# Normalisation, cosines and sines, and the first query weights ahead of an attention: a preparation stage rewritten

## The chip, the cores and the metric

The kernel runs on one core of one Trainium2 chip. The metric is the device time of one execution in microseconds, from the first to the last of its work on that core. TensorE multiplies, VectorE (DVE in the rows), ScalarE (ACT) and GpSimd (POOL) do element-wise work, and SyncE (SP) issues the transfers.

## What is computed

Four layers of a gated text model: for each, `x = x + tanh(g) * attention(layernorm(x))` and then `x = x + tanh(g) * ffn(layernorm(x))`. x has 32 x 64 tokens of 512 numbers (f32), which the kernel holds as 16 tiles of 128 tokens. The change lies at the entry of the fourth attention, which has 32 query heads and 8 key heads of size 128 and rotates queries and keys by their positions:

```python
cos_t, sin_t = _rope_tables(MAX_POS, D, ROPE_THETA)     # 512 positions x 128
cos = cos_t[position_ids][:, None]
sin = sin_t[position_ids][:, None]
q = q * cos + _rotate_half(q) * sin
k = k * cos + _rotate_half(k) * sin
...
scores = jnp.where(mask == 0, jnp.float32(-1000000000.0), scores)
```

In each table the second 64 columns repeat the first 64 (`concatenate([freqs, freqs])`).

## The kernel before

The program has four stages, one behind the other, each a block over all engines that ends in a barrier: `prepare_weights`, `early_layers` (three layers and their ffns, and the fourth attention's keys and values), `prepare_last` (L1489) and `last_attention` (L1641). `early_layers` leaves x in DRAM (`x_mid`), k and v too. Behind each stage GpSimd clears the stage's semaphores one by one (`stage`), and a barrier follows; at the start of the next, GpSimd raises the semaphores of the PSUM banks (`banks.open`, L277 and L278), two for each bank.

`prepare_last` fills what the last attention reads: `X` (x itself, 16 tiles), `xTh` and `xTl` (the normalised x, transposed and split into two bf16 halves), `cos` and `sin` (128 x 2048 f32, head dimension on the partitions), `mask`, and the first `raw_q` and `raw_o` (weights of the first four query heads). SyncE issues seven transfers in this order: the positions, copied to all 128 partitions; the table of cosines (512 x 128) and that of sines; all of x; the mask; raw_q; raw_o. VectorE turns positions to f32 and clamps them in four passes over 128 x 2048 (L1585 to L1591), and then makes four turns, each over four tiles (512 tokens). In a turn VectorE takes the statistics of four tiles (`bn_stats` L1604, `bn_aggr` L1607), GpSimd makes 1/sqrt(var + eps) for each tile in two operations (L1544, L1547), VectorE normalises (L1610, `xn`), TensorE transposes (L1565), ScalarE rounds to bf16 (L1577, `xTh`), and VectorE takes the rest (L1616, `xTl`). A position is looked up by a product: VectorE compares the positions with the row numbers (`hot`, L1599, four operations for a turn, into one buffer `one_hot`), and TensorE multiplies the table with that (L1558), in f32, cosines and then sines, each four products of 128x128 by 128x512; ScalarE copies the two results out (L1574). VectorE's order in a turn is statistics, normalise, `hot` of the next turn, `xTl`; TensorE's is cosines, sines, transposes. The mask comes last (L1626).

`last_attention` runs eight turns, one for each key head. Before its loop ScalarE rounds raw_q to `wqh` and GpSimd takes the rest, `wql`, in four pieces q0 to q3 (L1934, L2040). TensorE waits for q0's `wql` and projects queries (`project_q` by `three`, L349 to L351, twelve bf16 matmuls); VectorE multiplies by cos and sin (`rotate`, L2093 to L2095), and GpSimd adds the two parts (L2035). The list `FIRST` holds the projections and rotations that go ahead of the loop. From the second key head on, wqh and wql are made inside the loop, and this stays as it is.

## Time and profile before

| | us |
|---|---|
| median of 3 runs (2362.61 to 2378.12) | 2366.32 |
| the profiled execution, device time | 2366.56 |
| its span, first to last instruction | 2364.5 |
| TensorE busy | 1939.2 (82%) |
| VectorE busy | 1702.7 (72%) |
| ScalarE busy | 559.1 (24%) |
| GpSimd busy | 609.7 (26%) |
| granted TensorE clock, mean | 0.894 of full |

A row of the trace has a start and a duration in us from the span's start, the engine, the line of the kernel, the operation and, for a wait, how long the engine had been idle and what released it. `prepare_last` covers about 1244 to 1308 us of the span; TensorE's first matmul of the last attention stands at 1311.20 us.

### The profile page before, as it was taken

Reading aid. Unit: us, or ns where it says so; the run is one execution under the profiler, and the core shown is the slowest. Engines: PE = TensorE matmul, PEld = TensorE weight load, DVE = VectorE, ACT = ScalarE, POOL = GpSimd, SP = SyncE. Lnnn points to the kernel's source line nnn. Section 1 sums busy time; section 2 is a strip of 40 time slices with the busy share of each in tenths; the row PEclk is TensorE's granted clock in tenths of the full one; section 3 lists DMA queues with packets and bytes.
Section 4 is the critical chain, followed back from the end, with each engine's and each line's share of the span. In section 5 each row is a group of like instructions: output and inputs, shape, how many; then the busy total and the mean of one; then the engine's idle time right before and its main releaser. Section 6 shows DMA issues by size and latency. Waiting matters only on the chain. (4 is left out here: it accounts for less than half of the span.)

```text
span 2364.5 us, 40599 instructions
## 1 busy us (share of the span) xinstructions
PE 1939.2 (82%) x14722; PEld 1103.0 (47%) x14872; DVE 1702.7 (72%) x3005; ACT 559.1 (24%) x1326; POOL 609.7 (26%) x728
## 2 busy tenths in 40 slices
PE   4587879877898788887766798989899989898876
PEld 2343556435653455544543354545454545454432
DVE  4489655895459954698536788878788878887875
ACT  2221223222332223222221222222222222222221
POOL 0310213002230103201012434333334343434220
PEclk7699778997699986999857999999999999999987
DMA  7357202461043700453004212021212021200100
GB/s 228 134 139 202 63 2 82 125 188 54 1 127 111 204 8 1 131 158 106 1 18 142 72 28 62 28 61 27 63 28 62 27 62 27 62 27 27 31 24 36
DMA packets 134552, 176.08 MB, mean 74 GB/s; under 512 B 46304, under 2 KB 73568, under 8 KB 134288
## 3 DMA queue, kind: packets, MB, share of 16 engines
q1 hardware_dynamic: 134416, 174.20, 24.9%
q8 instruction: 94, 1.54, 0.3%
q14 instruction: 42, 0.34, 0.0%
HBM read 132.09 MB, written 42.07 MB: 74 GB/s over the span
## 5 line engine op out<-in xcount | busy, mean ns | idle before, releaser
L1122 POOL TENSOR_TENSOR early_vare<-early_mv,w_eps 128x1 f32<-128x1 f32 x96 | 31.3, 326 | 837.3 <-DVE early_mv L1187 823.0
L350 PE MATMUL la_ps<-w_xTl,la_wqh 128*128 128x512 bf16 x511 | 198.7, 389 | 13.5 <-POOL la_wql L2040 8.0
L2035 POOL TENSOR_TENSOR la_q<-la_straight,la_rot 128x512 f32<-128x512 f32 x128 | 164.2, 1283 | 175.3 <-DVE la_rot L2095 175.3
L350 PE MATMUL la_ps<-la_wol,la_oTh 128*128 128x512 bf16 x512 | 199.6, 390 | 6.2 <-issue 0.4
L349 PE MATMUL la_ps<-w_xTh,la_wqh 128*128 128x512 bf16 x504 | 197.6, 392 | 5.3 <-DVE la_rot L2095 4.6
L351 PE MATMUL la_ps<-la_woh,la_oTl 128*128 128x512 bf16 x511 | 198.2, 388 | 0.0
L351 PE MATMUL la_ps<-w_xTh,la_wql 128*128 128x512 bf16 x503 | 195.4, 388 | 0.1
L2048 POOL TENSOR_TENSOR la_p<-la_s,la_rec 128x256 f32<-128x256 f32 x128 | 92.9, 726 | 391.1 <-DVE la_rec L2116 390.5
L736 PE MATMUL early_ps<-early_products,w_heads 128*32 128x512 f32 x1024 | 132.1, 638 | 66.2 <-DVE early_products L1338 35.3
L349 PE MATMUL la_ps<-la_woh,la_oTh 128*128 128x512 bf16 x401 | 156.9, 391 | 10.8 <-DVE la_oTl L2123 9.1
L1939 ACT ACTIVATE la_s<-la_s 128x256 f32<-128x256 f32 x128 | 53.3, 417 | 421.4 <-DVE la_s L2109 421.4
L1985 ACT ACTIVATE la_oTh<-la_ps 128x256 bf16<-128x256 f32 x256 | 84.3, 381 | 286.1 <-PE la_ps L1894 286.1
L1338 DVE TENSOR_TENSOR early_products<-early_pR,early_vR 128x4096 f32<-128x4096 f32 x32 | 140.1, 4421 | 8.5 <-DMA early_pR<-scr_p 8.5
L1325 DVE TENSOR_TENSOR early_products<-early_qs,early_kp 128x4096 f32<-128x4096 f32 x32 | 140.0, 4417 | 0.0
L2130 DVE SCALAR_TENSOR_TENSOR w_X<-la_ps,w_gates,w_X 128x512 f32<-128x512 f32 x128 | 96.1, 751 | 57.8 <-PE la_ps L351 55.0
L641 PE MATMUL early_ps<-w_ident,early_xn 128*128 128x128 f32 x320 | 62.8, 349 | 87.2 <-DVE early_xn L1191 86.3
L1855 PE MATMUL la_ps<-la_k,la_q 128*64 128x64 f32 x2048 | 89.0, 230 | 43.4 <-POOL la_q L2035 39.1
L2093 DVE TENSOR_TENSOR la_straight<-la_ps,w_cos 128x512 f32<-128x512 f32 x128 | 88.4, 691 | 24.0 <-PE la_ps L351 22.7
L1894 PE MATMUL la_ps<-la_pT,la_v 64*128 64x128 f32 x1024 | 92.7, 298 | 14.5 <-ACT la_pT L1978 14.5
L2123 DVE TENSOR_TENSOR la_oTl<-la_ps,la_oTh 128x256 bf16<-128x256 f32 x256 | 96.0, 417 | 9.8 <-ACT la_oTh L1985 9.0
L1855 PEld LDWEIGHTS la_ps<-la_k,la_q 128*64 128x64 f32 x2048 | 71.3, 139 | 62.8 <-POOL la_q L2035 45.3
L1894 PEld LDWEIGHTS la_ps<-la_pT,la_v 64*128 64x128 f32 x1024 | 68.3, 187 | 65.4 <-issue 63.4
(329 smaller groups left out, 4619.3 us busy)
## 6 DMA issues: line engine op xcount, KB each, us to landing
early_vR<-scr_v SPq DMA_DIRECT2D x128, 257.0 KB, 5.0
early_wkv<-wkv SPq DMA_DIRECT2D x32, 512.0 KB, 4.1
la_v<-v SPq DMA_DIRECT2D x64, 256.0 KB, 3.8
k<-early_ctxt SPq DMA_DIRECT2D x32, 256.0 KB, 3.6
v<-early_ctxt SPq DMA_DIRECT2D x64, 128.0 KB, 2.8
scr_p<-early_weights SPq DMA_DIRECT2D x16, 512.0 KB, 2.6
early_pR<-scr_p SPq DMA_DIRECT2D x32, 256.0 KB, 3.5
w_raw_q<-in_Wq SPq DMA_DIRECT2D x8, 1024.0 KB, 6.4
```

The source lines that it names most:

```text
L349: pe.matmul(out, lh[c], rh[c], start=(first and c == 0), stop=False)
L350: pe.matmul(out, lh[c], rl[c], start=False, stop=False)
L351: ins = pe.matmul(out, ll[c], rh[c], start=False, stop=(last and c == n - 1))
L736: last = pe.matmul(out[32 * g:32 * g + 32, :], w["heads"][:, HEADS * (1 - odd):HEADS * (1 - odd) + 32], src(2 * g + odd), start=(opens and ...
L1325: qk_ready.send(dve.tensor_tensor(product[h][:, :, :, :], queries(j, h), keys_by_shift(j, h), ALU.mult))
L1338: pv_ready.send(dve.tensor_tensor(by_depth(j, h), pR[:, j % 2, h, :].unsqueeze(1).to_broadcast([P, CH, D]), vR[:, j % 2, :, h:h + D], ALU. ...
L1855: last = pe.matmul(out[SEQ * b:SEQ * b + SEQ, h * SEQ:(h + 1) * SEQ], q[:, m, h, cols], k[:, m, cols], start=True, stop=True, skip_group_c ...
L1894: last = pe.matmul(out[:, :, cols], v2[rows, m, u, b, :], pT[rows, u % 2, :, cols], start=True, stop=True)
L2035: rope_sum.send(pool.tensor_tensor(dst, straight[:, slot, :], rot[:, slot, :], ALU.add))
L2048: p_ready.send(pool.tensor_tensor(p[:, slot, :, :], s[:, slot, :, :], rec[:, slot, :].unsqueeze(2).to_broadcast([P, GROUP, SEQ]), ALU.mult))
L2123: banks.drain(dve.tensor_tensor(mine[0], banks.bank(name, n, u, *L)[:, 0:2 * P].rearrange("p (h t) -> p h t", h=2), mine[1], ALU.subtract) ...
L2130: banks.drain(dve.scalar_tensor_tensor(out=tile, in0=banks.bank("out", n, u, *L), scalar=w["gates"][:, 3:4], in1=tile, op0=ALU.mult, op1=A ...
```

## The change

`prepare_last` is written out without loops, in an order of its own for each engine.

- Transfers: positions, x tiles 0 to 3, one table, x tiles 4 to 7, raw_q, x tiles 8 to 11, x tiles 12 to 15, mask, raw_o. Each quarter of x has a semaphore of its own.
- One table of 512 x 128 holds 64 cosines and 64 sines, so a turn has one group of four f32 products (`rope`) and not two. ScalarE copies the upper half of the result to `cos[0:64]` and the lower to `sin[0:64]` (`half_rope`); GpSimd copies cos to the other 64 partitions and writes the negated sin there (`double`).
- The normalisation goes from VectorE to ScalarE: `scale * x + bias` with scale = rstd and bias = -mean * rstd. VectorE negates the four means, GpSimd makes vare, rstd and the new `offset` for four tiles at a time. `xn` has two buffers.
- The split of raw_q for the first key head moves from the start of `last_attention` to the end of `prepare_last` (`high_q` on ScalarE, a subtraction on GpSimd behind its last `double`). `wqh` and `wql` are kept across the two stages. SyncE raises `q_high` and `q_low` by four in their place at the start of `last_attention`.
- The stage has 37 semaphores in place of 26.

The diff, cut to its core:

```diff
-        vare, rstd = sb("vare", [P, QUAD]), sb("rstd", [P, QUAD])
...
-        row_ready = new_semaphore(nc, w, "pl_row_ready")
...
         def _(sp):
-            sp.dma_start(pos_raw[:, :], io["pos"].partition_broadcast(P)).then_inc(pos_loaded, 16)
-            sp.dma_start(table[:, 0, :, :], io["cos"].rearrange("(c p) n -> p c n", p=P)).then_inc(tables_loaded, 16)
-            sp.dma_start(table[:, 1, :, :], io["sin"].rearrange("(c p) n -> p c n", p=P)).then_inc(tables_loaded, 16)
-            sp.dma_start(w["X"][:, :, :], io["x_mid"].rearrange("(t p) n -> p t n", p=P)).then_inc(x_loaded, 16)
-            sp.dma_start(mask_raw[:, :, :], io["mask"].rearrange("(t p) n -> p t n", p=P)).then_inc(mask_loaded, 16)
-            load_q(sp, io, w, 0).then_inc(heads_loaded, 16)
-            load_o(sp, io, w, 0).then_inc(heads_loaded, 16)
-            sp.wait_ge(heads_loaded, 32)
+            def load_x(t):
+                x_loaded[t].send(sp.dma_start(
+                    w["X"][:, quad(t), :], io["x_mid"][t * PER:(t + 1) * PER, :].rearrange("(t p) n -> p t n", p=P)))
+
+            pos_loaded.send(sp.dma_start(pos_raw[:, :], io["pos"].partition_broadcast(P)))
+            load_x(0)
+            table_loaded.send(sp.dma_start(table[:, :, :], io["rope"].rearrange("(c p) n -> p c n", p=P)))
+            load_x(1)
+            q_loaded.send(load_q(sp, io, w, 0))
+            load_x(2)
+            load_x(3)
+            mask_loaded.send(sp.dma_start(mask_raw[:, :, :], io["mask"].rearrange("(t p) n -> p t n", p=P)))
+            o_loaded.send(load_o(sp, io, w, 0))
+            sp.wait_ge(o_loaded.sem, 16)
...
-            pool.iota(row[:, :], pattern=[[P, C]], base=0, channel_multiplier=1,
...
-            with pool.Fori(0, TURNS) as turn:
-                for j in range(QUAD):
-                    stats_ready.wait(pool, turn, j)
-                    pool.tensor_tensor(vare[:, j:j + 1], mv[:, j, 1:2], w["eps"][:, :], ALU.add)\
-                        .then_inc(pool_step, 1)
-                    pool.wait_ge(pool_step, turn * QUAD + (j + 1))
-                    rstd_ready.send(pool.tensor_tensor(rstd[:, j:j + 1], vare[:, j:j + 1], w["power"][:, 0:1],
-                                                       ALU.pow))
...
+            def rstd_of(t):
+                pool.wait_ge(stats_ready.sem, t + 1)
+                moments.send(pool.tensor_tensor(vare[:, quad(t)], mv[:, quad(t), 1],
+                                                w["eps"][:, :].to_broadcast([P, QUAD]), ALU.add))
+                pool.wait_ge(moments.sem, t + 1)
+                rstd_ready.send(pool.tensor_tensor(rstd[:, quad(t)], vare[:, quad(t)],
+                                                   w["power"][:, 0:1].to_broadcast([P, QUAD]), ALU.pow))
+                pool.wait_ge(rstd_ready.sem, t + 1)
+                offset_ready.send(pool.tensor_tensor(offset[:, quad(t)], mv[:, quad(t), 0], rstd[:, quad(t)],
+                                                     ALU.mult))
+
+            def double(t):
+                pool.wait_ge(half_ready.sem, 2 * t + 2)
+                pool.wait_ge(offset_ready.sem, min(t + 3, TURNS))
+                doubled.send(pool.tensor_copy(w["cos"][64:128, tokens(t)], w["cos"][0:64, tokens(t)]))
+                pool.wait_ge(doubled.sem, 2 * t + 1)
+                doubled.send(pool.tensor_scalar(w["sin"][64:128, tokens(t)], w["sin"][0:64, tokens(t)], -1.0, None,
+                                                ALU.mult))
+                pool.wait_ge(doubled.sem, 2 * t + 2)
+
+            rstd_of(0)
+            rstd_of(1)
+            rstd_of(2)
+            double(0)
+            rstd_of(3)
+            double(1)
+            double(2)
+            double(3)
+            for h in range(GROUP):
+                cols = slice(h * HD, (h + 1) * HD)
+                pool.wait_ge(q_high.sem, h + 1)
+                q_low.send(pool.tensor_tensor(w["wql"][:, :, cols], w["raw_q"][:, :, cols], w["wqh"][:, :, cols],
+                                              ALU.subtract))
+            pool.wait_ge(q_low.sem, GROUP)
...
-            pe.wait_ge(tables_loaded, 32)
-            with pe.Fori(0, TURNS) as turn:
-                for k, step in enumerate(("cos", "sin")):
-                    hot_ready.wait(pe, turn, QUAD - 1)
-                    banks.wait_free(pe, turn, step)
...
+                    last = pe.matmul(banks.bank("rope", t), table[:, c, :], one_hot[:, c, :],
...
+            def turn_x(t):
+                for j in range(QUAD):
+                    pe.wait_ge(xn_ready.sem, t * QUAD + j + 1)
+                    banks.wait_free(pe, 0, "turn", t, j)
...
+            for t in range(TURNS):
+                turn_x(t)
+                rope(t)
...
-            with act.Fori(0, TURNS) as turn:
-                for k, step in enumerate(("cos", "sin")):
-                    banks.wait_filled(act, turn, step)
-                    banks.drain(act.activation(w[step][:, bass.ts(turn, PER)], banks.bank(step), ACT.Copy), step)
-                for j in range(QUAD):
-                    banks.wait_filled(act, turn, "turn", j)
...
+            def normalise(t):
...
+                    i = t * QUAD + j
+                    xn_ready.send(act.activation(xn[:, t % 2, j, :], w["X"][:, i, :], ACT.Identity,
+                                                 scale=rstd[:, i:i + 1], bias=offset[:, i:i + 1]))
...
+            def high(t):
+                for j in range(QUAD):
+                    banks.wait_filled(act, 0, "turn", t, j)
+                    i = t * QUAD + j
...
+            def half_rope(t):
+                banks.wait_filled(act, 0, "rope", t)
+                half_ready.send(act.activation(w["cos"][0:64, tokens(t)], banks.bank("rope", t)[0:64, :], ACT.Copy))
+                last = act.activation(w["sin"][0:64, tokens(t)], banks.bank("rope", t)[64:128, :], ACT.Copy)
+                banks.drain(last, "rope", t)
+                banks.wait_drained(act, 0, "rope", t)
+                act.sem_inc(half_ready.sem, 1)
...
+            normalise(0)
+            normalise(1)
+            high(0)
+            half_rope(0)
+            normalise(2)
+            high(1)
+            half_rope(1)
+            normalise(3)
+            high(2)
+            half_rope(2)
+            act.wait_ge(q_loaded.sem, 16)
+            high_q(0)
+            high_q(1)
+            high(3)
+            half_rope(3)
+            high_q(2)
+            high_q(3)
...
-            apart = Apart(dve, row_ready, 1)
...
+            def statistics(t):
+                dve.wait_ge(x_loaded[t].sem, 16)
...
+                    dve.bn_stats(stats[:, i, :], w["X"][:, i, :]).then_inc(counted.sem, 1)
...
+                dve.wait_ge(gathered.sem, t * QUAD + QUAD)
+                negated.send(dve.tensor_scalar(mv[:, quad(t), 0], mv[:, quad(t), 0], -1.0, None, ALU.mult))
+                dve.wait_ge(negated.sem, t + 1)
+                dve.sem_inc(stats_ready.sem, 1)
...
+            def hot(t):
+                if t >= 1:
+                    banks.wait_filled(dve, 0, "rope", t - 1)
                 for c in range(C):
-                    hot_ready.send(dve.tensor_scalar(one_hot[:, c, :], pos[:, bass.ts(turn, PER)],
-                                                     row[:, c:c + 1], None, ALU.is_equal))
...
-            def body(turn, more):
-                for j in range(QUAD):
-                    dve.bn_stats(stats[:, j, :], w["X"][:, bass.ds(turn * QUAD + j, 1), :]).then_inc(dve_step, 1)
-                for j in range(QUAD):
-                    apart.wait_ge(dve_step, turn * QUAD + (j + 1))
-                    stats_ready.send(dve.bn_aggr(mv[:, j, :], stats[:, j, :]))
...
-                    rstd_ready.wait(dve, turn, j)
-                    xn_ready.send(dve.tensor_scalar(xn[:, j, :], w["X"][:, bass.ds(turn * QUAD + j, 1), :],
-                                                    mv[:, j, 0:1], rstd[:, j:j + 1], ALU.subtract, ALU.mult))
-                if more:
-                    hot(turn + 1)
...
-                    xT_high.wait(dve, turn, j)
...
+            dve.wait_ge(pos_loaded.sem, 16)
+            once.send(dve.tensor_copy(pos[:, :], pos_raw[:, :]))
+            dve.wait_ge(once.sem, 1)
+            once.send(dve.tensor_scalar(wrap[:, :], pos[:, :], 0.0, float(POSITIONS), ALU.is_lt, ALU.mult))
+            dve.wait_ge(once.sem, 2)
+            statistics(0)
+            once.send(dve.tensor_tensor(pos[:, :], pos[:, :], wrap[:, :], ALU.add))
+            dve.wait_ge(once.sem, 3)
+            once.send(dve.tensor_scalar(pos[:, :], pos[:, :], 0.0, float(POSITIONS - 1), ALU.max, ALU.min))
+            dve.wait_ge(once.sem, 4)
+            dve.wait_ge(row_ready.sem, 1)
+            statistics(1)
             hot(0)
-            dve.wait_ge(x_loaded, 16)
-            with dve.Fori(0, TURNS - 1) as turn:
-                body(turn, True)
-            body(TURNS - 1, False)
-            dve.wait_ge(mask_loaded, 16)
+            statistics(2)
+            low(0)
+            hot(1)
+            statistics(3)
+            low(1)
+            hot(2)
+            low(2)
+            hot(3)
+            dve.wait_ge(mask_loaded.sem, 16)
             dve.tensor_scalar(w["mask"][:, :, :], mask_raw[:, :, :], 0.0, MASKED, ALU.is_equal, ALU.mult)
+            low(3)
...
-        wqh, wql = sb("wqh", [P, C, GROUP * HD], HALF), sb("wql", [P, C, GROUP * HD], HALF)
+        wqh, wql = w["wqh"], w["wql"]
...
             sp.sem_inc(o_loaded.sem, 16)
+            sp.sem_inc(q_low.sem, len(PIECES))
+            sp.sem_inc(q_high.sem, len(PIECES))
...
             for place, which, step in FIRST:
                 if which is not None:
-                    q_low.wait(pe, 0, PIECES.index(f"q{which}"))
                     project_q(0, place, step, which)
...
-            for piece in PIECES:
-                high_of(piece)
             exponentials(0, 0, 0)
             with act.Fori(0, KV - 1) as turn:
...
-            for piece in PIECES:
-                low_of(0, 0, piece)
             for i, (place, which, step) in enumerate(FIRST):
                 add_rotation(0, place, i % 2, rotated(which, step))
...
@@ -2333,7 +2423,7 @@
```

## Rows read from the trace of the kernel before

**Rows 1.** Page, first part: busy us (share of span) and instructions by engine.

```profile
PE 1939.2 (82%) x14722; PEld 1103.0 (47%) x14872; DVE 1702.7 (72%) x3005; ACT 559.1 (24%) x1326; POOL 609.7 (26%) x728
```

**Rows 2.** Timeline behind the stage: start us, us, engine, operation, [idle <-releaser].

```profile
1305.14 0.68 DVE L1626 TENSOR_SCALAR w_mask<-pl_mask 128x1024 bf16<-128x1024 int32 x1
1308.20 2.19 ACT L1934 ACTIVATE la_wqh<-w_raw_q 128x512 bf16<-128x512 f32 x4 [4.03 <-PEq L72]
...
1309.59 4.48 POOL L2040 TENSOR_TENSOR la_wql<-w_raw_q,la_wqh 128x512 bf16<-128x512 f32 x4
...
1311.20 0.63 PE L350 MATMUL la_ps<-w_xTl,la_wqh 128*128 128x512 bf16 x1 [7.95 <-POOL la_wql L2040]
```

**Rows 3.** By line, 1236 to 1308: xcount | busy us, mean ns | idle.

```profile
L1558 PE MATMUL pl_ps<-pl_one_hot,pl_table 128*128 128x512 f32 x64 | 32.9, 673 | 27.1 <-DVE pl_one_hot L1599 27.1
...
L1547 POOL TENSOR_TENSOR pl_rstd<-pl_vare,w_power 128x1 f32<-128x1 f32 x16 | 11.2, 701 | 1.3
L1616 DVE TENSOR_TENSOR w_xTl<-pl_ps,w_xTh 128x512 f32 (+1 forms) x16 | 9.9, 683 | 0.9 <-ACT w_xTh L1577 0.9
L1604 DVE BATCH_NORM_STATS2 pl_stats<-w_X 128x6 f32 (+1 forms) x16 | 9.9, 680 | 5.3 <-DMA w_X<-x_mid 5.3
...
L1577 ACT ACTIVATE w_xTh<-pl_ps 128x512 f32 x16 | 9.0, 600 | 2.0 <-PE pl_ps L1565 2.0
L1610 DVE TENSOR_SCALAR pl_xn<-w_X,pl_mv,pl_rstd 128x512 f32 (+1 forms) x16 | 8.7, 546 | 8.2 <-POOL pl_rstd L1547 8.2
...
L1599 DVE TENSOR_SCALAR pl_one_hot<-pl_pos,pl_row 128x512 f32 (+1 forms) x16 | 6.7, 481 | 0.0
L1544 POOL TENSOR_TENSOR pl_vare<-pl_mv,w_eps 128x1 f32<-128x1 f32 x16 | 3.0, 187 | 40.7 <-DVE pl_mv L1607 40.7
...
L1607 DVE BATCH_NORM_AGGREGATE pl_mv<-pl_stats 128x2 f32<-128x6 f32 x16 | 1.5, 155 | 0.0
```

**Rows 4.** Transfers of the stage: size in KB, median us from issue to landing.

```profile
w_X<-x_mid SPq DMA_DIRECT2D x1, 4096.0 KB, 16.2
```

**Rows 5.** Timeline of the stage: its start, second turn and a later table look-up.

```profile
1244.31 0.35 SPq L1527 DMA_DIRECT2D pl_pos_raw<-in_pos  x1
...
1249.13 1.23 DVE L1585 CAST pl_pos<-pl_pos_raw 128x2048 f32<-128x2048 int32 x1 [13.05 <-DMA pl_pos_raw<-in_pos]
...
1251.65 2.29 DVE L1589 TENSOR_TENSOR pl_pos<-pl_pos,pl_wrap 128x2048 f32<-128x2048 f32 x1
...
1262.20 2.47 DVE L1604 BATCH_NORM_STATS2 pl_stats<-w_X 128x6 f32 x4 [5.29 <-DMA w_X<-x_mid]
...
1270.92 7.13 PE L1558 MATMUL pl_ps<-pl_one_hot,pl_table 128*128 128x512 f32 x16 [1.01 <-DVE pl_one_hot L1599]
...
1277.89 1.04 PE L1565 MATMUL pl_ps<-w_ident,pl_xn 128*128 128x128 f32 x8
...
1292.67 8.82 PE L1558 MATMUL pl_ps<-pl_one_hot,pl_table 128*128 128x512 f32 x16 [1.01 <-DVE pl_one_hot L1599]
```

**Rows 6.** Stretches: PE, PEld, DVE, ACT, POOL busy, granted clock, DMA share, GB/s.

```profile
1255.00:1262.00 7.00, 4.95 (x6) 2.19 (x7) 1.88 (x5) 0.00 (x0) 0.00 (x0) 0.50 1.07 377
...
1293.00:1296.00 3.00, 3.00 (x5) 1.17 (x4) 3.00 (x6) 0.00 (x0) 0.00 (x0) 0.52 0.00 0
```

**Rows 7.** By line, whole span: ScalarE with a scale, and a GpSimd copy.

```profile
L1101 ACT ACTIVATE early_osb<-early_ps,w_gates 128x512 f32<-128x512 f32 x16 | 11.0, 688 | 40.3 <-PE early_ps L915 40.3
...
L1104 ACT ACTIVATE early_xTh<-early_xTf 128x512 bf16<-128x512 f32 x16 | 9.9, 620 | 0.0
...
L162 POOL CAST w_identh<-w_ident 128x128 bf16<-128x128 f32 x1 | 0.3, 289 | 0.1
```

**Rows 8.** Timeline, one GpSimd addition beside VectorE's multiplications.

```profile
1315.67 0.69 DVE L2094 TENSOR_TENSOR la_rot<-la_ps,w_sin 64x512 f32<-64x512 f32 x1
...
1317.14 1.77 POOL L2035 TENSOR_TENSOR la_q<-la_straight,la_rot 128x512 f32<-128x512 f32 x1 [3.06 <-DVE la_rot L2095]
...
1317.80 1.66 DVE L2094 TENSOR_TENSOR la_rot<-la_straight_k,w_sin 64x512 f32<-64x512 f32 x1
```

More of the change, by code:

```diff
@@ L1492, in prepare_last @@
     plan = []
[L1493 to L1495 removed]
+    for t in range(TURNS):
+        for j in range(QUAD):
+            plan.append((("turn", t, j), j))
+        plan.append((("rope", t), 4 + t % 2))
     with ExitStack() as ctx:
@@ L1550, in _ @@
+            pool.wait_ge(q_low.sem, GROUP)
         @block.tensor
         def _(pe):
-            pe.wait_ge(tables_loaded, 32)
-            with pe.Fori(0, TURNS) as turn:
-                for k, step in enumerate(("cos", "sin")):
-                    hot_ready.wait(pe, turn, QUAD - 1)
-                    banks.wait_free(pe, turn, step)
-                    for c in range(C):
-                        last = pe.matmul(banks.bank(step), table[:, k, c, :], one_hot[:, c, :],
-                                         start=(c == 0), stop=(c == C - 1))
-                    banks.fill(last, step)
-                for j in range(QUAD):
-                    xn_ready.wait(pe, turn, j)
-                    banks.wait_free(pe, turn, "turn", j)
-                    for c in range(C):
-                        last = pe.transpose(banks.bank("turn", j)[:, c * P:(c + 1) * P],
-                                            xn[:, j, c * P:(c + 1) * P], w["ident"][:, :])
-                    banks.fill(last, "turn", j)
+            pe.wait_ge(table_loaded.sem, 16)
@@ new lines, in rope @@
+            def rope(t):
+                pe.wait_ge(hot_ready.sem, t + 1)
+                banks.wait_free(pe, 0, "rope", t)
+                for c in range(C):
+                    last = pe.matmul(banks.bank("rope", t), table[:, c, :], one_hot[:, c, :],
+                                     start=(c == 0), stop=(c == C - 1))
+                banks.fill(last, "rope", t)
+            def turn_x(t):
+                for j in range(QUAD):
+                    pe.wait_ge(xn_ready.sem, t * QUAD + j + 1)
+                    banks.wait_free(pe, 0, "turn", t, j)
+                    for c in range(C):
+                        last = pe.transpose(banks.bank("turn", t, j)[:, c * P:(c + 1) * P],
+                                            xn[:, t % 2, j, c * P:(c + 1) * P], w["ident"][:, :])
+                    banks.fill(last, "turn", t, j)
@@ new lines, in high @@
+            def high(t):
+                for j in range(QUAD):
+                    banks.wait_filled(act, 0, "turn", t, j)
+                    i = t * QUAD + j
+                    xT_high.send(act.activation(w["xTh"][:, :, i * P:(i + 1) * P],
+                                                banks.bank("turn", t, j).rearrange("p (c n) -> p c n", c=C), ACT.Copy))
+            def half_rope(t):
[5 more added lines that the diff above has]
+                act.sem_inc(half_ready.sem, 1)
@@ new lines, in high_q @@
+            def high_q(h):
+                cols = slice(h * HD, (h + 1) * HD)
+                q_high.send(act.activation(w["wqh"][:, :, cols], w["raw_q"][:, :, cols], ACT.Copy))
+            normalise(0)
[11 more added lines that the diff above has]
+            high_q(1)
@@ L1612, in body @@
-                if more:
-                    hot(turn + 1)
-                for j in range(QUAD):
-                    xT_high.wait(dve, turn, j)
-                    banks.drain(dve.tensor_tensor(w["xTl"][:, :, bass.ts(turn * QUAD + j, P)],
-                                                  banks.bank("turn", j).rearrange("p (c n) -> p c n", c=C),
-                                                  w["xTh"][:, :, bass.ts(turn * QUAD + j, P)], ALU.subtract),
-                                "turn", j)
@@ L2282, in build @@
                 keep(attention, name, shape)
+            for name in ("wqh", "wql"):
+                keep(attention, name, [P, C, GROUP * HD], HALF)
             keep(attention, "cos", [P, TOKENS])
```

77 lines of the change are left out of this document (42 added, 35 removed).

## The prediction

> **What bounds the kernel now.** The page first: no engine is full. TensorE is busy 82% of the span, VectorE 72%, ScalarE and GpSimd about a quarter [rows 1]. That is an average over four stages with barriers between them, so what the change is worth has to be read inside `prepare_last` and at the seam behind it. The timeline of the seam [rows 2] gives the two marks that I reckon with: the last operation of the stage, the mask, starts at 1305.14 and ends at 1305.82, and the last attention's first matmul starts at 1311.20. Nothing of the later stages is changed, so each microsecond by which that first matmul comes earlier is one off the total. Between the two marks lie 2.38 us until ScalarE starts (26 semaphores cleared, barrier), and then 3.00 us in which TensorE waits for the first piece of `wql`; the row names that releaser.
>
> Inside the stage, the groups by line [rows 3] show a chain and not a full engine. The stage starts at 1244.31 [rows 5]. VectorE waits 5.3 us for x, GpSimd waits 40.7 us for means, TensorE 27.1 us for `one_hot`. VectorE has the most: its rows sum to 9.9 + 9.9 + 8.7 + 6.7 + 1.5 us, with the passes over the positions and the mask 43. TensorE's look-up products take 32.9 us, and one turn's sixteen instructions 7.13 us at the full clock [rows 5]. A turn lasts some 11 us (second look-up 1270.92, fourth 1292.67, two turns between them): statistics, GpSimd, normalise, transposes and xTl follow one another.
>
> **The transfers.** x comes as one transfer, lands 16.2 us after its issue [rows 4], and VectorE's first statistics start at 1262.20 [rows 5]. The engines of the DMA are full then, at 377 GB/s [rows 6]. The positions land at 1249.1 (VectorE starts at 1249.13). A quarter of x is 1.05 MB, 2.8 us at that rate: the first lands at 1251.9, and with the 0.2 to 0.3 us until an engine starts, statistics can begin at 1252.1. The same rate, with the table, raw_q and the other quarters in their order, gives 1255.6, 1261.2 and 1264.0; none of these three holds VectorE up. raw_q is there by 1258.4 and is first needed at 1284; mask and raw_o land by about 1270.
>
> **Durations.** Four `bn_stats` take 2.47, four `bn_aggr` 0.37 (from the timeline [rows 5] and the mean of the group [rows 3]). The added negation has no row; the nearest, bn_aggr at 155 ns, gives 0.16 and about 0.2 for its waits, with 0.1 and 0.5 as ends. So a block of statistics is 3.2. `hot` is 1.67, xTl four times 0.62 = 2.49, rounding to xTh 0.53 each back to back. A normalisation on ScalarE lies between 620 (from SBUF) and 688 ns (with a scale) [rows 7]; I take 0.62, since rows start before the last ends. GpSimd's power over four numbers is 0.55 if the width is free and 1.63 if each costs 0.36 more than the addition at 0.19 [rows 3]; I take 1.0, and at either end the sum below stays. Its look-up half, eight instructions, is 3.5 at full clock and 6.8 at half (six took 4.95 at a clock of 0.50, [rows 6]). Sixteen transposes are 2.1 at the full clock (eight 1.04) and 4.3 at half. `double` is two operations on 64x512; the copy of 128x128 took 289 ns [rows 7], the addition of 128x512 1.27 when alone. With a fixed part of 0.1 the first gives 0.86; the ends are 0.5 and 1.27. Two make 1.7, with 1.1 and 2.6 as ends.
>
> **The new order, step by step.** VectorE: two passes over positions to 1251.6, statistics(0) 1252.1 to 1255.3, two more passes (2.33 + 1.25) to 1258.9, statistics(1) to 1262.0, hot(0) to 1263.7, statistics(2) to 1266.9. ScalarE normalises the first four tiles from 1257.0, TensorE turns them cold until 1262.0. rope(0) runs 1263.8 to 1270.6 if cold, to 1267.2 if warm; before, the clock rose only after some 5 us of unbroken matmuls from 1257.05, and here there are 4.3 us and a gap of 1.8, so I take it cold. It costs the sum only 1.4, as xTl of turn 0 fills the rest.
>
> Then each engine waits for another: hot(1) to 1272.5, transposes(1) to 1272.7, rope(1) to 1276.1. Meanwhile ScalarE does half_rope(0) (to 1272.0), normalise(2) (1274.5), xTh of turn 1 (1276.6), and so VectorE's xTl(1) ends at 1278.1, hot(2) at 1279.8, rope(2) at 1283.3, hot(3) at 1285.1, transposes(3) at 1285.4, rope(3) at 1288.8. Behind this hangs a tail that did not exist: half_rope(3) 1.4 (1290.2), double(3) 1.8 (1292.0), and on GpSimd, in front of which double(3) stands, all four subtractions for `wql`. They took 4.48 together [rows 2], and end at 1296.5. ScalarE's pieces of wqh are ready by 1291.3 and hidden; VectorE is through at 1288.9. At the full clock a period is 7.2 us against about 11: the saved look-up (3.5), the normalisation and GpSimd's eight turns of hand account for it.
>
> Before, the clock fell once in the stage, while TensorE was busy: the fourth look-up took 8.82 in place of 7.13 [rows 5], at a clock of 0.52 [rows 6]. With less work for TensorE I expect at least one such fall, 1.7 us: the stage ends at 1298.2, against 1305.82.
>
> **The seam.** 2.38 us for 26 semaphores bounds one clearing at 0.09; eleven more are 0.9 (nothing at the least, if the barrier is all of it). 1298.2 + 2.4 + 0.9 = 1301.5. TensorE then needs only the bank that GpSimd raises, 0.2 us, since nothing waits for wql: 1301.7 against 1311.20, 9.5 us. The 3.0 us at the start of the last attention are thus not saved in full: 4.5 us of subtraction are paid in the tail of the stage instead, because GpSimd does them last. The eight semaphore counts that SyncE adds stand ahead of k's load; k is read only behind the first query's projection and rotation, which cover them; without that cover they cost 0.1. The first matmuls are cold before and after.
>
> Sum, on the profiled execution: 2366.56 - 9.5 = 2357.1. The median lies 0.24 below that execution, so for the median 2356.8; I give 2357.
>
> **Rivals.**
> 1. *The clock stays at half.* What speaks for it: TensorE is less filled, and it fell once before at 0.52. Against: at half clock its own work fills the turn, which lets the clock rise. With every look-up at 6.8 and transposes at 4.3, TensorE becomes the bound, 11.1 us a turn; rope(3) ends at 1304.1, the stage at 1311.7, the first matmul at 1315.2: 4.0 us later than before, 2370. This is the case on the other side. It decides once 9.5 us more than the one fall are lost: all three later look-ups cold (10) with their transposes.
> 2. *GpSimd and VectorE slow each other.* One addition on GpSimd took 1.77 while VectorE's multiplication of two SBUF inputs took 1.66 in place of 0.69 [rows 8]. Here double(1) stands beside hot(2), and the others beside hot or xTl. If each hot loses 1.2, the stage ends 4.2 later: 2361. The Trainium skill, "GPSIMD Engine Reference", section Key points, says that the two share their SBUF interfaces and contend when VectorE's instruction uses two ports or has two SBUF inputs. The trace agrees for the second case (1.66 against 0.69); for `hot`, one input, no row here shows it, and by that rule the result would be this rival's 2361.
> 3. *x by quarters is no earlier.* If the first statistics still start at 1262.20, the stage ends 8.7 later at the same clock: 2366, no change. For it: the trace has no landing of a part of x. Against: the positions, issued first, landed at 1249.1 with all the others behind them, so the queue serves them in order.
> 4. *A gain over 1%* (23.7 us) needs the first matmul at 1287.5. VectorE alone has, from 1249.13, 12.8 + 6.7 + 10.0 + 6.8 = 36 us left, so 1285.4 and the seam, 1288.9. Only a disturbance elsewhere gives it.
>
> **How the numbers follow.** Forecast 0.62, clock at half 0.12, contention 0.12, quarters no earlier 0.08, else 0.06. The low end: no fall (1.7), warm rope(0) (1.4), cheap copies (0.6), power, negation and seam at their lower ends (1), and 3.7 by which the lowest run of before lies under its median: 2349. The high end takes in contention and late quarters: 2366. Some 0.8 lies inside. A change of 1% is about what a measurement here can tell from none. The forecast is 0.4% and all rivals with a place lie within 1%, so: faster 0.06, same 0.91, slower 0.03, the small shares for drift elsewhere (before's runs spread over 15.5 us).
>
> **What would show it.** First statistics at about 1252; first look-up at 1263.8, the last ending at 1289 to 1291; normalisations on ScalarE of 0.6 us; on GpSimd two copies of 0.5 to 1.3 us and then four subtractions of 1.1 as the stage's last work; the first matmul of the last attention 0.2 us after the barrier, at 1300 to 1303; from there on the same intervals as before. It is wrong if a period is 11 us (clock), if x lands at 1262, if GpSimd's power over four numbers takes several microseconds, or if the later stages move.

## The result and the profile after

| | before | after |
|---|---|---|
| median of seven runs, us | 2366.32 | 2391.32 (2385.99 to 2394.33) |
| ratio | | 1.0098, 95% interval 1.0077 to 1.0119 |
| span of the profiled execution, us | 2364.5 | 2390.3 |
| granted TensorE clock, mean | 0.894 | 0.887 |

The changed kernel is 25 us slower; 2357 was forecast. Ratios, here and below, are to the kernel before measured beside the same run (its medians lie between 2366.3 and 2370.6). First the stage itself, in the timeline of the kernel after (start us, us, engine, line, operation, idle before and releaser):

```profile
1252.81 0.35 SPq L1538 DMA_DIRECT2D pl_pos_raw<-in_pos  x1
...
1260.67 2.47 DVE L1669 BATCH_NORM_STATS2 pl_stats<-w_X 128x6 f32<-128x512 f32 x4 [1.02 <-DMA w_X<-x_mid]
...
1280.49 3.70 PE L1598 MATMUL pl_ps<-pl_one_hot,pl_table 128*128 128x512 f32 x8 [1.48 <-DVE pl_one_hot L1684]
...
1293.85 3.70 PE L1598 MATMUL pl_ps<-pl_one_hot,pl_table 128*128 128x512 f32 x8
...
1298.96 0.61 POOL L1569 COPY w_cos<-w_cos 64x512 f32<-64x512 f32 x1 [2.53 <-issue]
1299.65 1.48 POOL L1571 TENSOR_SCALAR w_sin<-w_sin 64x512 f32<-64x512 f32 x1
1301.22 4.48 POOL L1586 TENSOR_TENSOR w_wql<-w_raw_q,w_wqh 128x512 bf16<-128x512 f32 x4
...
1309.55 0.63 PE L350 MATMUL la_ps<-w_xTl,w_wqh 128*128 128x512 bf16 x1 [11.99 <-POOLq L278]
```

The stage starts at 1252.81 here and 1244.31 before [rows 5]: the early layers, whose code is the same, ended 8.5 us later. Over the profiles of this study the stage's start lies anywhere from 1242.9 to 1259.2, so I count from its start. The first matmul of the last attention comes 56.7 us after it (1309.55 - 1252.81); before it was 66.9 (1311.20 - 1244.31, [rows 2, 5]). The rewritten stage is thus 10.2 us shorter. The last attention takes it back, and more: from its first matmul to the end of the span 1080.8 us, against 1053.3 before, 27.5 more. Together the later start (8.5), the stage (-10.2) and the attention (27.5) are the 26 us between the two spans.

The place is the step from one turn of its loop over key heads to the next. TensorE in the timeline after:

```profile
1447.77 0.38 PE L351 MATMUL la_ps<-la_woh,la_oTl 128*128 128x512 bf16 x1
1450.82 0.32 PE L1949 MATMUL la_ps<-la_k,la_q 128*64 128x64 f32 x3 [2.67 <-issue]
1453.79 0.91 PE L1949 MATMUL la_ps<-la_k,la_q 128*64 128x64 f32 x13 [2.65 <-issue]
1454.64 0.61 PE L349 MATMUL la_ps<-w_xTh,w_wqh 128*128 128x512 bf16 x1
1455.04 0.63 PE L350 MATMUL la_ps<-w_xTl,w_wqh 128*128 128x512 bf16 x1
```

And the same place before:

```profile
1449.18 0.38 PE L351 MATMUL la_ps<-la_woh,la_oTl 128*128 128x512 bf16 x1
1449.49 0.69 PE L1855 MATMUL la_ps<-la_k,la_q 128*64 128x64 f32 x16
1450.11 0.39 PE L349 MATMUL la_ps<-w_xTh,la_wqh 128*128 128x512 bf16 x1
```

Two holes of 2.7 us whose releaser is `issue`: TensorE waited for nothing that the profile shows. The matmuls behind them take 0.61 to 0.63 in place of 0.38, because the granted clock has fallen to half (PE, PEld, DVE, ACT, POOL busy, granted clock, DMA share, GB/s):

```profile
1454.00:1457.00 3.00, 3.00 (x19) 1.40 (x17) 1.69 (x4) 0.88 (x3) 0.00 (x0) 0.50 0.00 0
```

The DMA queues of that stretch (1438 to 1458; packets, MB, share), after:

```profile
q8 instruction: 2, 0.03, 0.7%
```

q8 is a queue that brings instructions. Narrower windows place its two packets, the first in 1447.5 to 1448.5, the second in 1451 to 1452:

```profile
q8 instruction: 1, 0.02, 8.3%
```

```profile
q8 instruction: 1, 0.02, 6.0%
```

One starts where the first hole begins (1448.15), the other where the second does (1451.14). Before has no line of q8 in 1438 to 1458. Over the whole span (the page's part 3), before and after:

```profile
q8 instruction: 94, 1.54, 0.3%
```

```profile
q8 instruction: 140, 2.29, 0.4%
```

A packet is 16,384 bytes (2.29 MB / 140). In the last attention (from SyncE's first issue on) 25 packets fall before and 70 after, there 9 in each of its inner turns; before, five of its six measured turns have none and one has 9. As a measure for each turn I take the time from SyncE's issue for `raw_q` (end of a turn) to that for `raw_o` (start of the next), called the back edge below:

```profile
1446.13 0.39 SPq L1723 DMA_DIRECT2D w_raw_q<-in_Wq  x1
...
1463.92 0.38 SPq L1729 DMA_DIRECT2D w_raw_o<-in_Wo  x1
```

That is 17.8 us. The six back edges that can be measured so are 17.2 to 18.8 after (sum 108.9), and before 11.8 to 12.1 with a single 16.6 (sum 76.7): 32 us more. The remainders of the turns sum to 633.7 after and 636.8 before, so nothing else got longer.

### The profile page after: what moved, and what is told of

Read it like the earlier page. It is cut to its first block and busy times, and to the rows that moved or that the text cites. A ratio compares the mean times of both kernels' runs of the same rounds, so it can differ in the third digit from the quotient of the medians.

```text
span 2390.3 us, 40387 instructions
## 1 busy us (share of the span) xinstructions
PE 1937.8 (81%) x14690; PEld 1103.7 (46%) x14840; DVE 1695.9 (71%) x2993; ACT 570.4 (24%) x1342; POOL 615.7 (26%) x716
## 3 DMA queue, kind: packets, MB, share of 16 engines
q8 instruction: 140, 2.29, 0.4%
## 5 line engine op out<-in xcount | busy, mean ns | idle before, releaser
L350 PE MATMUL la_ps<-w_xTl,w_wqh 128*128 128x512 bf16 x511 | 202.1, 395 | 17.8 <-POOLq L278 12.0
L349 PE MATMUL la_ps<-w_xTh,w_wqh 128*128 128x512 bf16 x504 | 200.8, 398 | 5.7 <-DVE la_rot L2184 4.5
L351 PE MATMUL la_ps<-w_xTh,w_wql 128*128 128x512 bf16 x503 | 197.5, 393 | 0.2 <-issue 0.2
L736 PE MATMUL early_ps<-early_products,w_heads 128*32 128x512 f32 x1024 | 139.2, 670 | 64.3 <-DVE early_products L1338 34.3
L736 PEld LDWEIGHTS early_ps<-early_products,w_heads 128*32 128x32 f32 x1024 | 29.9, 116 | 146.3 <-issue 81.3
```

Of the source, the lines that this page charges most:

```text
L349: pe.matmul(out, lh[c], rh[c], start=(first and c == 0), stop=False)
L350: pe.matmul(out, lh[c], rl[c], start=False, stop=False)
L351: ins = pe.matmul(out, ll[c], rh[c], start=False, stop=(last and c == n - 1))
L736: last = pe.matmul(out[32 * g:32 * g + 32, :], w["heads"][:, HEADS * (1 - odd):HEADS * (1 - odd) + 32], src(2 * g + odd), start=(opens and ...
```

## The experiments

The probe is padding that computes nothing: waits of TensorE on a semaphore that has long been raised, at the start of `prepare_last`. By the same count two waits make one instruction.

**1. The changed kernel, loop moved by 127 instructions, to 35.25 to 41.88.**

```diff
+            for _ in range(254):
+                pe.wait_ge(banks.drained[0], 1)
             pe.wait_ge(table_loaded.sem, 16)
```

> The changed kernel with 127 instructions more on TensorE, all waits on a semaphore that is raised already, at the start of prepare_last, where TensorE idles for 16 us. TensorE's loop of the last attention then starts 256 instructions behind where it started in the kernel before; counted in blocks of 256 instructions from the start of TensorE's program it runs from 35.25 to 41.88 (before: 34.25 to 40.88, seven blocks; changed: 34.76 to 41.38, eight). Theory F (instruction fetch): the changed kernel loses its time at the loop's back edges because TensorE's loop lies over eight blocks and its instructions are read again in each turn; here the seven back edges cost what they cost before, the instruction queue moves 94 packets of 16 KB and not 140, and the time is 2391 - 29 - (0 to 8) = 2354 to 2363. Theory M (memory or signals: wqh and wql lie elsewhere now and q_low is raised by SyncE): nothing of that is touched, 2391.

2366.18 us, 0.9978 (0.9956 to 1.0001) of before. Four back edges of 12.1, two of 16.0 and 16.4; 34 packets in the last attention, 104 in all. The time is 3 us over the forecast and the packets 10 more, by those two turns, but the loss is gone, with nothing but waits added: the attention's new entry and its transfers are as they were.

**2. The kernel before, moved by 129, to the changed kernel's place, 34.76 to 41.38.**

```diff
+            for _ in range(258):
+                pe.wait_ge(banks.drained[0], 1)
             pe.wait_ge(tables_loaded, 32)
```

> The kernel before with 129 instructions more on TensorE at the start of prepare_last, of the same kind. Its last loop then lies as in the changed kernel, 34.76 to 41.38. Theory F: each back edge of the last attention costs 6 us more, 2366 + 29 = 2395 (2388 to 2402), and the instruction queue moves about 140 packets of 16 KB. Theory M: no change, 2366.

2396.51 us, 1.0097 (1.0066 to 1.0128); 70 packets, back edges of 17.5 to 19.2. The loss appears in the old code, so it is no part of what the change computes.

**3. Control: the same 254 waits on VectorE.**

```diff
+            for _ in range(254):
+                dve.wait_ge(banks.drained[0], 1)
             dve.wait_ge(pos_loaded.sem, 16)
```

> Control: the changed kernel with the same 127 instructions on VectorE, at the start of prepare_last where it waits for the positions. Theory F: TensorE's loop stays at 34.76 to 41.38, so 2391 (2384 to 2396) and 140 packets. If what counts is the place of VectorE's loop (279 instructions) or the size of the whole program, the time differs from that.

2393.7 us, 1.0089 (1.0058 to 1.012); 70 packets, back edges of 17.3 to 18.3. The waits were not hidden (the stage got 7.6 us longer), yet the loss stayed: it is TensorE's program that counts.

**4. Moved by 64** (`range(128)` on TensorE), to 35.01 to 41.63, measured three times.

> The changed kernel with 64 instructions more on TensorE: the loop runs from 35.01 to 41.63, seven blocks again. Theory F in its sharp form (what counts is how many blocks the loop touches): fast, 2354 to 2363, 94 packets. If only the same place as before (modulo a block) is good, or if blocks are counted from another origin by more than a few instructions: slow, 2391.

> The changed kernel with 64 instructions more on TensorE, again and in more rounds (TensorE's last loop from 35.01 to 41.63 blocks). The prediction without the loop: 9.5 us below a kernel before whose loop lies alike. Theory F with the occasional back edge of 16.5 us in place of 12.1 (seen in 1 of 6, 2 of 6 and 0 of 6) as the cause of the scatter: 2352 to 2366, median about 2361.

> The changed kernel with 64 waits, a third time, beside e11 and the kernel before. Expected 2355 to 2362 us, a ratio of 0.994 to 0.998, 86 packets, back edges of 12.1. If the turns of 107.2 us come by chance, the split of 105.6 and 107.2 among its turns differs from the first two profiles of it (three and four turns of 107.2).

2363.53, 2357.42 and 2357.09 us: 0.9978 (0.9953 to 1.0003), 0.9947 (0.9926 to 0.9968) and 0.9941 (0.9918 to 0.9964). All back edges 12.1 to 12.2, 16 packets (86 in all, where 94 were forecast). The last two show the gain of the rewritten stage: 10 to 12 us, and times of 2357.

**5. The kernel before, moved by 193 to the same place** (`range(386)`).

> The kernel before with 193 instructions more on TensorE at the start of prepare_last, so that its last loop lies at 35.01 to 41.63 blocks too, seven blocks as before and ending at the same place of a block as in e9. Theory F: no 6 us at the back edges, 2366 to 2371; e9 is then 9.5 us below it, which is the change alone. If the padding itself costs (193 instructions at 60 ns, 11.6 us, against 12 us of idle time), up to 3 us more.

2376.20 us, 1.0036 (1.0023 to 1.005), 5 us over the forecast; back edges and packets as in 4. These waits outlast TensorE's idle time:

```profile
1271.47 2.07 PE L1560 MATMUL pl_ps<-pl_one_hot,pl_table 128*128 128x512 f32 x2 [32.93 <-issue]
```

and the stage is 69.4 us in place of 63.9. Less these 5.5 the kernel before would be at 2370.7 here, the changed one at 2357.4: 13 us apart. The traces show 7.5 for the stage (56.4 against 63.9) and 2.6 for the attention's first matmul (0.3 us behind SyncE's first issue, against 2.95); the rest of the 13 is not assigned.

**6. Where exactly is the border?** Moved by 16, 48, 160, 240 and 320 (`range(32)` to `range(640)`).

> The changed kernel with 48 TensorE waits at the start of prepare_last instead of 64: sixteen fewer, and nothing else differs from the fast one with 64. Counted in blocks of 256 TensorE instructions, the loop of the last attention now runs from 34.95 to 41.57, so it touches eight blocks again, where the one with 64 (35.01 to 41.63) touches seven. Theory F (a loop that touches eight blocks is fetched anew in every turn): slow as the changed kernel, about 2388 to 2394 us, about 140 packets of 16384 bytes on the instruction queue, back edges of 17 to 19 us. Rival (the waits' own time, or a smooth effect of where the code lies, does it): within 4 us of the kernel with 64, about 2357 to 2364, with some 86 packets and back edges of 12.1.

> The changed kernel with 160 waits: more than in any fast version of it, the loop from 35.38 to 42.01, eight blocks again, by two or three instructions of the eighth. Theory F: slow, about 2388 to 2396 us with some 140 packets, unless the last few instructions of the loop as counted are not needed for the turn (the count is good to a few instructions), in which case 2358 to 2366 with 86 to 104 packets. Rival (more waits make it faster, as by a delay that helps): about 2357 to 2366 and 86 packets or so. A gap of 2 us either way is not told apart from the time that the waits themselves take.

> The changed kernel with 16 more TensorE instructions (32 waits) at the start of prepare_last. By the measured fast one with 48 and the measured slow one with 160, the counted positions are 14 to 31 instructions too low, and the loop then runs from block 34.88 to 34.95 up to 41.50 to 41.57: eight blocks. Blocks theory: slow, 2388 to 2394 us, 140 packets, back edges of 17 to 19 us. Rival (any padding at all moves something else, a few instructions are enough): 2350 to 2362 us and 86 packets.

> The changed kernel with 240 more TensorE instructions: the loop, with the correction of 14 to 31, from 35.75 to 35.82 up to 42.37 to 42.44, eight blocks of 256. Blocks theory: 140 packets, back edges of 17 to 19 us. The 480 waits take longer than TensorE is idle at the start of the stage (193 instructions cost 5.5 us in the kernel before), so the stage gets some 8 us longer and the time of 2396 to 2404 says less than the packets and back edges. Rival (a limit that is passed once, so that either all longer programs are slow or the loss is gradual): also slow; this run tells it apart only together with the one with 320.

> The changed kernel with 320 more TensorE instructions, 256 more than the fast one with 64: the loop moved on by exactly one block, 36.07 to 36.13 up to 42.69 to 42.75, seven blocks. Blocks theory (where the loop lies within a block of 256 decides, with a period of 256): fast again in the last attention, 86 packets (or 87, one block more in all), back edges of 12.1 us, though the stage is some 12 us longer by the 640 waits, so about 2360 to 2372 us in all. Rival (the slow cases with 160 and 240 come from the program's length): slow, 140 packets and more, back edges over 14 us, 2390 to 2405 us.

| moved by | loop as counted | packets in the attention | back edges, us | us | ratio (95%) |
|---|---|---|---|---|---|
| 0 | 34.76 to 41.38 | 70 | 17.2 to 18.8 | 2391.32 | 1.0098 |
| 16 | 34.82 to 41.44 | 16 | 12.1 | 2359.18 | 0.9949 (0.9919 to 0.9979) |
| 48 | 34.95 to 41.57 | 16 | 12.1 | 2356.21 | 0.9955 (0.9925 to 0.9984) |
| 64 | 35.01 to 41.63 | 16 | 12.1 | 2357 to 2364 | see 4 |
| 127 | 35.25 to 41.88 | 34 | 12.1, two of 16 | 2366.18 | 0.9978 |
| 160 | 35.38 to 42.01 | 70 | 14.4 to 15.3 | 2368.05 | 1.0009 (0.9985 to 1.0033) |
| 240 | 35.70 to 42.32 | 69 | 17.1 to 17.9 | 2391.99, once | |
| 320 | 36.01 to 42.63 | 16 | 12.1 | 2373.10, once | |

The forecasts for 16 and 48 were missed: 16 instructions already cure the loss. 160 fell between its two forecasts, with the packets of the slow one and nearly the time of the fast one. The one with 320 tells most. It is 256 more than the 64 of experiment 4, later in the program than the slow ones with 160 and 240, and its back edges are fast again, with one packet more in the whole span:

```profile
q8 instruction: 87, 1.43, 0.2%
```

(86 with 64. The 640 waits make its stage 18 us longer and account for 2373.10, 1 us over the forecast.) So the program's length is no cause, and the place within a block of 256 is. But the count is not exact. Shifts of 16 to 127 are fast, 0 and 160 slow: a width of 112 to 159 places. A loop of 1696 instructions would leave only 97 places in which it touches seven blocks; 112 to 159 belong to one of 1634 to 1681. My count of the loop is 15 to 62 too long, and its start at least 45 too low. With that the blocks theory holds for every kernel here; without it, it fails at 16 and 48. Which instructions are counted wrongly wasn't found. So the corrected count is fitted to these runs and was not tested by a further one.

A slow turn brings 9 packets, one more than the eight blocks that the loop touches. A reading that fits, and that no run tested: one block is always fetched ahead, and there is room for eight. Seven touched and one ahead then stay loaded, eight and one don't.

At 160 all 70 packets come, but a back edge costs 2.5 us and not 6. Its trace shows one hole, the one with 240 two:

```profile
1451.92 0.69 PE L1951 MATMUL la_ps<-la_k,la_q 128*64 128x64 f32 x16 [2.74 <-issue]
1457.67 0.69 PE L1951 MATMUL la_ps<-la_k,la_q 128*64 128x64 f32 x16
```

```profile
1456.44 0.56 PE L1951 MATMUL la_ps<-la_k,la_q 128*64 128x64 f32 x11 [2.69 <-issue]
1459.15 0.49 PE L1951 MATMUL la_ps<-la_k,la_q 128*64 128x64 f32 x5 [2.15 <-issue]
```

**7. The tail in another order:** wqh and wql of the first heads between `half_rope(2)`, `double(2)` and `double(3)`, on the kernel with 64.

```diff
+            double(1)
+            low_q(0)
+            low_q(1)
+            pool.wait_ge(q_low.sem, 2)
             double(2)
+            low_q(2)
+            low_q(3)
+            pool.wait_ge(q_low.sem, 4)
             double(3)
```

> The changed kernel with the 64 instructions more on TensorE, and its tail spread: ScalarE rounds pieces 0 and 1 of raw_q ahead of half_rope(2) and 2 and 3 behind it, GpSimd subtracts 0 and 1 ahead of double(2) and 2 and 3 ahead of double(3), where it was idle for 5.4 and 2.5 us. Theory T (the last thing of the stage is GpSimd's 4.48 us of subtraction, and nothing hides it): the stage is 4.5 us shorter, less 0.7 us if a subtraction slows VectorE's hot(3), so prep from first issue to the next stage's first issue 56.4 - 3.8 = 52.6 us, and the time 4 us under that of e9. Rival: VectorE and ScalarE are slowed as much by the subtractions beside them as the tail gains; prep 55 to 57 us, no change.

2359.91 us, 0.9959 (0.9942 to 0.9976). The stage is 53.6 us, 2.8 less than the kernel with 64. 3.8 less was forecast, 4.5 for the subtractions less 0.7 for a slower comparison; VectorE's comparison beside GpSimd's subtraction lost 1.7 (1.68 alone):

```profile
1297.69 2.46 POOL L1583 TENSOR_TENSOR w_wql<-w_raw_q,w_wqh 128x512 bf16<-128x512 f32 x2 [3.26 <-ACT w_wqh L1652]
```

```profile
1298.51 3.42 DVE L1693 TENSOR_SCALAR pl_one_hot<-pl_pos,pl_row 128x512 f32<-128x512 f32 x4 [0.43 <-PE pl_ps L1607]
```

In the time nothing of it is to be seen (2357.42 with 64 beside it, the intervals overlap); experiment 8 names what can hide it.

**8. The first split put back into the last attention**, moved by 60 so that the loop runs from 35.01 to 41.64, twice, the second time beside the third measurement of 4.

```diff
-            high_q(0)
-            high_q(1)
             high(3)
             half_rope(3)
-            high_q(2)
-            high_q(3)
...
+            for piece in PIECES:
+                high_of(piece)
```

> The changed kernel, its loop placed alike (35.01 blocks, 60 instructions more), with one part undone: raw_q is split at the start of last_attention again, as before. The prediction's step has the move pay 4.5 us in the stage's tail and save 3.0 us of TensorE's wait: without it the stage is 4.5 us shorter (51.9 us), the first matmul stands 3.0 us behind the stage's end, not 0.3, and the time is 1.5 us under that of e9. If the move is worth what its removal from the front of the last attention suggests, it is 3 us above e9.

> The same kernel as the one with the first split of the query weights put back into the last attention (and 60 waits), a second time beside e12. Against the kernel before: expected at a ratio of 0.993 again, about 2350 us. Theory G (moving the split lengthens the stage more than it shortens the attention: 4.7 us against 3.0): 1.7 us under e12. Theory H (it was the turns of 107.2 us instead of 105.6 that made 2350 in the first measurement, and those come by chance): within 2 us of e12 at any sign. Told apart from both: 5 us or more under e12 again would mean that the split's place changes the later turns too.

2350.56 us, 0.9927 (0.9904 to 0.995), and 2346.93 us, 0.9912 (0.9885 to 0.9939): 7 and 10 us under the kernel with 64 beside it, the fastest of the study, and more than theory G or H allowed. The stage is 51.7 and 52.1 us (56.4 with the split). The attention, from SyncE's first issue to the end, is 1045.1 in the second, 3.3 longer than the 1041.8 of the kernel with 48, whose turns are otherwise equal. So putting the split back gains about 1 us (theory G). The rest is TensorE's clock, which theory H only had as turns of two lengths. In most versions some turns last 107.2 us from `raw_o` to the next `raw_q` and others 105.6. They part at one place, after the same gap of 1.8 us. The stretches of 4 us behind it in a turn of each kind, of the kernel with 64 (second measurement; PE, PEld, DVE, ACT, POOL busy, granted clock, DMA share, GB/s):

```profile
1468.35:1472.35 4.00, 4.00 (x34) 2.19 (x33) 2.59 (x7) 0.80 (x2) 0.61 (x1) 1.00 0.00 0
1586.05:1590.05 4.00, 4.00 (x25) 1.71 (x24) 1.87 (x5) 0.42 (x1) 0.61 (x1) 0.58 0.00 0
```

and their matmuls in the timeline:

```profile
1468.20 0.69 PE L1951 MATMUL la_ps<-la_k,la_q 128*64 128x64 f32 x16 [1.77 <-POOL la_q L2128]
1468.82 0.39 PE L349 MATMUL la_ps<-w_xTh,w_wqh 128*128 128x512 bf16 x1
...
1585.89 0.69 PE L1951 MATMUL la_ps<-la_k,la_q 128*64 128x64 f32 x16 [1.76 <-POOL la_q L2128]
...
1588.05 0.63 PE L350 MATMUL la_ps<-w_xTl,w_wqh 128*128 128x512 bf16 x1
```

The clock fell to 1.2 GHz in one turn and stayed at 2.4 GHz in the other, for the same work and the same gap. A fall costs 1.6 us. It came in all six turns of the third measurement's profile, in five of the second's, in four of the first's, in six of experiment 7's, in three with 16 and three in the kernel before, in none with 48, and in none of the two profiles with the split put back. Six falls are 9.6 of the 12.3 us between the third measurement's attention (1054.1) and that with 48 (1041.8). Whether the split's place keeps the clock up, or these profiles had luck, two profiles don't settle; the one with 48 kept it without moving the split.

## Why the prediction was wrong, and where it was right

- **The step that failed** is in the first part: that nothing of the later stages is changed, "so each microsecond by which that first matmul comes earlier is one off the total". What they compute is unchanged, where their code lies is not. The term that is missing from the sum is +27.5 us (1080.8 - 1053.3), and experiments 1, 2 and 6 show that the loop's place makes it. The profiled execution lies 35 us over the forecast of 2357.1: this term, 8.5 by which the early layers ended later, and less than 1 the other way in the stage. The diff held the shift, 129 instructions of TensorE more by unrolling; the profile held the size of a block (1.54 MB in 94 packets), and hints of a fetch in the one back edge of 16.6. Neither said that the new place is a bad one: 16 instructions further it is a good one. No rival had a mechanism that reaches past the stage; "if the later stages move" stands among the signs of being wrong, without one.
- The Trainium skill, "Runtime: NRT & Kernel Launch", section "Instruction fetch mechanics", gives TensorE's instruction memory as 128 KiB, refilled in blocks of 256 instructions, and says that a taken branch to a page outside the window stalls. The packets of 16,384 bytes and the holes at the back edge agree. By its window of two pages every turn of the kernel before would fetch as well; here five of the six measured did not, so for such a loop the measurement decides. By the capacity alone (2048 instructions, eight blocks) the loop would have fitted in either place; with one block fetched ahead, the reading of experiment 6, only in the place with seven.
- **The stage was right, in part by luck:** 52.9 us to its last operation (1305.70 - 1252.81) against 53.9 forecast, first statistics 7.9 after its start (7.8), last look-up done 44.7 after it (44.5), the four subtractions 4.48 as the last work, and 3.5 for the seam until SyncE's first issue (3.3). First matmul 10.2 earlier; 9.5 was forecast. The end fits so well because terms that were too long and terms that were too short cancelled.
- With the loop in a good place the changed kernel measures 2356.2 to 2363.5 when moved by 16, 48 or 64; the forecast of 2357 is a time of this stage with such a loop.
- **Its terms** were off in both directions. No fall of the clock came (1.7 forecast); in the profile of the kernel with 48 one did, a look-up took 5.40 in place of 3.70, and that stage is 58.4 us and not 56.4. The first look-up took 4.40, with 6.8 forecast for the half clock and 3.5 for the full. Normalisation took 0.73 each (2.93 for four) and not 0.62; the pair of copies 2.2 to 2.9 and not 1.7.
- **Contention** (rival 2) came, small: two comparisons of four beside GpSimd's copies took 2.37 and 2.48 in place of 1.67, so the group has 574 ns in place of 481 [rows 3]. After, by line:

```profile
L1684 DVE TENSOR_SCALAR pl_one_hot<-pl_pos,pl_row 128x512 f32<-128x512 f32 x16 | 8.2, 574 | 0.6 <-PE pl_ps L1598 0.4
L1571 POOL TENSOR_SCALAR w_sin<-w_sin 64x512 f32<-64x512 f32 x4 | 6.3, 1578 | 0.3
L1557 POOL TENSOR_TENSOR pl_vare<-pl_mv,w_eps 128x4 f32<-128x4 f32 x4 | 3.0, 740 | 17.2 <-DVEq L1678 17.2
```

- **Clock at half** (rival 1) and **quarters no earlier** (rival 3) did not come: the three later look-ups took 3.70 each, at the full clock, and x's first quarter 7.9 us after the start.

## What to carry to other kernels

Before a loop is unrolled, count by engine what that adds ahead of every later loop that is long (here some 1640 to 1680 instructions), and compare the packets of the instruction queue before and after: an eighth block of 256 touched by this loop cost some 6 us in most places, 2.5 in one, in each turn. Where the profile says `issue` at a loop's back edge and instruction packets come in each turn, a few idle instructions ahead of it tell in one run whether the place is at fault. And an edit's gain is only known once the loop behind it lies equally well in both kernels; here the same edit reads as 25 us lost or 10 us won.

## What the runs showed of the hardware beyond that

- The kernel before and the changed one moved by 127, whose loops lie alike within a block, fetch in some turns all the same: 9 packets and a back edge of 16.0 to 16.6, in one and two turns of six. Their loop ends at most 32 instructions short of a block's end (127 is still fast, 160 isn't). None of the kernels moved by 16, 48, 64 or 320, whose loop ends at least 63 instructions short of it, did so.
- A GpSimd addition over 128x4 numbers took 0.20 us alone and 2.36 beside VectorE's addition of two inputs over 128x2048, and ended when VectorE did:

```profile
1263.77 2.36 POOL L1557 TENSOR_TENSOR pl_vare<-pl_mv,w_eps 128x4 f32<-128x4 f32 x1 [9.86 <-DVEq L1678]
1263.77 2.29 DVE L1701 TENSOR_TENSOR pl_pos<-pl_pos,pl_wrap 128x2048 f32<-128x2048 f32 x1
```

- On GpSimd a multiplication by a constant over 64x512 took 1.48 us where a copy of that size took 0.61, and 254 waits on a raised semaphore cost VectorE 7.6 us.
